# Attention loop of a Perceiver-style block: VectorE forms the low half of the softmax weights in every slot, GpSimd keeps the division and the copies of queries

## The reference, cut to what matters

```python
kv_rope = kv_c * cos + rotate_half(kv_c) * sin          # 4096 x 128, shared by all heads
q_r = einsum('bshq,hqr->bhsr', q_big, W_qr)             # 256 x 64 per head
k_r = einsum('bld,hdr->bhlr', kv_rope, W_kr)            # 4096 x 64 per head
scores = einsum('bhsr,bhlr->bhsl', q_r, k_r)
attn = softmax(scores, axis=-1)
ctx_c = einsum('bhsl,bld->bhsd', attn, kv_rope)         # 256 x 128 per head
```

## Time and profile before

| | before |
|---|---|
| median of 3 runs | 714.37 us (714.17 to 716.49) |
| the profiled execution, its own time | 717.11 us |
| its span, first to last instruction | 715.2 us |
| mean granted TensorE clock | 0.967 of 2.4 GHz |
| TensorE busy | 651.5 us (91%) |
| VectorE busy | 392.3 us (55%) |
| ScalarE busy | 365.5 us (51%) |
| GpSimd busy | 192.4 us (27%) |

### The profile page before, as it was taken

One profiled execution on the slowest core, in us unless ns is written; L12 is line 12 of the kernel. 1 busy time (PEld: TensorE's weight loads), 2 busy tenths in 40 slices (PEclk: granted clock), 3 DMA queues, 4 the chain that ended last, 5 costly groups with the idle time before them and its releaser, 6 DMA issues.

```text
span 715.2 us, 14853 instructions
## 1 busy us (share of the span) xinstructions
PE 651.5 (91%) x5860; PEld 457.7 (64%) x5860; DVE 392.3 (55%) x541; ACT 365.5 (51%) x540; POOL 192.4 (27%) x154
## 2 busy tenths in 40 slices
PE   5899899999999999999999999989978988898457
PEld 4776576777777777777777777985556856632111
DVE  1977677767767767767777675341137836100001
ACT  2453476677666676667577666861217842110000
POOL 2430134343443434344334334440002210000000
PEclk9999999999999999999999999999999989999768
DMA  8914691423324224224306215009970051399990
GB/s 362 418 51 95 144 335 41 108 45 70 77 49 88 49 49 88 53 46 99 76 12 132 51 32 113 2 10 416 417 288 1 0 207 60 136 397 419 416 391 34
DMA packets 25112, 105.13 MB, mean 147 GB/s; under 512 B 3697, under 2 KB 6897, under 8 KB 19185
## 3 DMA queue, kind: packets, MB, share of 16 engines
q1 hardware_dynamic: 25072, 104.57, 44.7%
HBM read 77.29 MB, written 0.52 MB: 109 GB/s over the span
## 4 chain that ended last, share of the span: by engine, by line
PE 61%; DVE 17%; issue 9%; DMA 6%; ACT 4%; SPq 3%; POOL 1%; DVEq 0%; ACTq 0%
DVE arena L748 8%; PE psO L1040 6%; PE psM L989 6%; DMA arena<-w_exp 6%; PE psO L1031 5%; PE psO L1032 5%; PE psS L1018 5%; PE psS L1019 5%; PE psO L1111 4%; DVE arena L711 3%; SPq L374 3%; PE psO L944 3%; PE psO L976 2%; PE psS L1253 2%; PE psO L978 2%
## 5 line engine op out<-in xcount | busy, mean ns | idle before, releaser
L711 DVE TENSOR_REDUCE arena<-psM 128x2 f32<-128x1024 f32 x128 | 156.7, 1224 | 79.4 <-PE psM L989 79.2
L440 POOL TENSOR_TENSOR arena<-arena 128x1024 bf16<-128x1024 f32 x64 | 138.4, 2163 | 144.7 <-ACT arena L539 140.6
L538 ACT ACTIVATE arena<-psS 128x1024 bf16<-128x1024 f32 x128 | 132.2, 1032 | 26.0 <-PE psS L1019 13.8
L1031 PE MATMUL psO<-arena 128*128 128x129 bf16 x1024 | 132.8, 220 | 1.5 <-ACT arena L538 1.2
L539 ACT ACTIVATE arena<-psS 128x1024 f32<-128x1024 f32 x128 | 132.5, 1035 | 0.0
L1032 PE MATMUL psO<-arena 128*128 128x128 bf16 x1024 | 132.3, 220 | 0.0
L1018 PE MATMUL psS<-arena 128*128 128x256 bf16 x512 | 120.5, 273 | 1.4 <-DVE arena L722 1.4
L1019 PE MATMUL psS<-arena 65*128 65x256 bf16 x512 | 120.8, 273 | 0.0
L1031 PEld LDWEIGHTS psO<-arena 128*128 128x128 bf16 x1024 | 99.1, 98 | 20.9 <-issue 12.7
L1032 PEld LDWEIGHTS psO<-arena 128*128 128x128 bf16 x1024 | 99.3, 97 | 6.7
L748 DVE TENSOR_TENSOR arena<-arena 128x1024 bf16<-128x1024 f32 x64 | 82.2, 1285 | 20.7 <-ACT arena L539 20.7
(11 more groups left out here) (192 smaller groups left out, 766.8 us busy)
## 6 DMA issues: line engine op xcount, KB each, us to landing
arena<-w_exp SPq DMA_DIRECT2D x32, 1024.0 KB, 17.3
arena<-arena SPq DMA_DIRECT2D x96, 256.0 KB, 3.8
arena<-w_exp SPq DMA_DIRECT2D x32, 512.0 KB, 17.9
arena<-w_pair SPq DMA_DIRECT2D x8, 1088.0 KB, 16.6
arena<-w_o SPq DMA_DIRECT2D x1, 4096.0 KB, 21.1
arena<-ctx SPq DMA_DIRECT2D x4, 512.0 KB, 13.4
arena<-rope SPq DMA_DIRECT2D x4, 512.0 KB, 14.1
arena<-w_shared_in SPq DMA_DIRECT2D x1, 2048.0 KB, 8.7
```

The lines of the kernel that those rows point to most:

```text
L440: nc.gpsimd.tensor_tensor(p_lo[:, s % 2, :], p_f[:, s % 2, :], p_hi[:, s % 2, :], ALU.subtract).then_inc(s_plo[0], 1)
L538: nc.scalar.activation(p_hi[:, s % 2, :], psS[s % 2][:, :], ACT.Exp).then_inc(s_phi, 1)
L711: nc.vector.reduce_max(maxes[:, :, st, c], psM[:, :].rearrange("p (j n) -> p j n", j=2), AX.X).then_inc(s_mfree, 1)
L1031: mm(psC[:, st, :], ph, vx[:, GROUP * g + i, 0:CW], start=g == 0 and i == 0 and st == 0, stop=False, skip_group_check=True)
```

## The change

GpSimd no longer forms p_lo; VectorE forms it in even slots as well, at the place in its slot where it did so in odd ones, and each parity's semaphore is incremented from there. GpSimd keeps normalise, bring_next and bring, which now follow each other with no p_lo between them. TensorE gets one more wait in slot 0 of a pair: the maximum of keys piece 1 waits for bring's copies by name (it used to be sure of them through the p_lo of slot 14).

```diff
-            def low_part(p, s):
-
-                wait_apart(pool, s_pf, p * SLOTS + s + 1, pool_passed)
-                wait_apart(pool, s_pv, p * SLOTS + s - 1, pool_passed)
-                nc.gpsimd.tensor_tensor(p_lo[:, s % 2, :], p_f[:, s % 2, :], p_hi[:, s % 2, :], ALU.subtract).then_inc(s_plo[0], 1)
...
                     if s == HALF:
                         normalise(p * 2)
-                    low_part(p, s)
                     if after and s == 4:
                         bring_next(p + 2)
...
                     for d, m in maxima[0:1]:
                         maximum(p + d, m)
-                    if s % 2:
-                        dve.wait_ge(s_pf, t + 1)
-                        wait(dve, s_pv, t - 1)
-                        nc.vector.tensor_tensor(p_lo[:, s % 2, :], p_f[:, s % 2, :], p_hi[:, s % 2, :], ALU.subtract).then_inc(s_plo[1], 1)
+                    dve.wait_ge(s_pf, t + 1)
+                    wait(dve, s_pv, t - 1)
+                    nc.vector.tensor_tensor(p_lo[:, s % 2, :], p_f[:, s % 2, :], p_hi[:, s % 2, :], ALU.subtract).then_inc(s_plo[s % 2], 1)
                     for d, c in keys:
                         keys_low(p + d, c)
...
                 if st == 0:
                     pe.wait_ge(s_khi, q * CHUNKS + c + 1)
+                if m == TT and not (isinstance(q, int) and q < 2):
+                    pe.wait_ge(qmax_copied, q * 3 + 3)
```

## The result

The changed kernel takes 725.09 us (median; 723.45 to 727.45), the kernel before 714.27 us beside it: 1.0153 times, 95% interval 1.0111 to 1.0194. That is 10.8 us slower, where 13.8 were forecast; 728.2 us was the forecast time, and 725.1 lies in the range of 720 to 736. One execution of the kernel before (1045.85 us) and one of e3 (1250.09 us) were slow ones and stand in no comparison.

A forecast was written before the change was run, and what follows sets the result against it. A ring of waits between VectorE and TensorE was taken to bound the kernel. ENTRY 4.4, pairs 1 to 5 6.2, pair 6 0.7 and copies 2.5 sum to 13.8 us over the 714.4 median: 728.2 us, range 720 to 736.

The forecast's parts named there:

- the ring: Loop's double slots: VectorE and TensorE wait on each other in 6.31 us; work between even and odd reductions free to 2.89.
- case A: The prediction's own case: VectorE becomes the bound in the late reductions, 11 to 18 us more; chance 0.70.
- Plain double slots: Slots 2, 4, 6 and 10 of a pair: even to odd reduction becomes 2.93 for 2.89 us, taken as +0.03.
- Slots 0 and 8: Slots where a finished head is copied out first: odd reduction at 2.93 for 2.66 us, +0.26, twice per pair.
- Slots 12 to 15: Late slots of a pair: from p_lo of slot 13 to that of slot 15, 6.62 for 6.02 us, +0.6.
- The copies' meeting: Slot 0: GpSimd's bring_next copies delay VectorE's subtraction 0.5 us on five pairs, 2.5 us, from 0 to 3.6.
- ENTRY: First stretch: slots 4 and 6 +0.91 each, 8 and 10 +0.59 each, 0 +0.6, 3 +0.2, 12 to 15 +0.6; 4.4 us.
- Pairs 6 and 7: Last pairs: pair 6, two head slots' terms, four plain ones, no tail, 0.7 us; pair 7, no reductions, 0.
- rival D: Faster: GpSimd is slower, so moving gives back ScalarE's waits and pair 7's two meetings, to 706.6 us; chance 0.06.
- Dispatch: Loop's double slots, pairs 1 to 5: register waits might add 0 to 0.1 us each, up to 4 us; taken 0.
- rival B: VectorE bounds every slot and costs more, with dispatch and all copies going first: 733 to 736 us; chance 0.15.
- Rival C: Loop's double slots absorb the subtraction and the tail; only ENTRY's single psM shows, 3 to 5 us; chance 0.06.

The follow-up runs named there:

- e3: Changed kernel with GpSimd's copies of bring_next after the division of slot 8 rather than in front of it; 725.26 us beside 714.61, ratio 1.0161.
- e1: Kernel before, with VectorE taking the even subtraction only in plain slots 2, 4, 6, 10 of pairs 1 to 6; 714.55 us beside 714.61, ratio 0.9998.
- e2: Changed kernel, but GpSimd keeps the even subtraction in slots 2, 4, 6, 10 of pairs 1 to 6; 725.86 us beside 714.61, ratio 1.0151.
- e5: Changed kernel with VectorE's subtraction ahead of the reduction in odd slots only; 714.39 us beside 713.92, ratio 1.0009.
- e8: e5 plus ScalarE making the high keys of even slots 0 to 10 behind the next slot's exponentials, outside ENTRY; 711.41 us beside 714.41, ratio 0.9965.
- e7: Kernel before, odd subtraction ahead of its reduction, ScalarE's high keys of even slots 0 to 10 behind next slot's exponentials outside ENTRY; 706.26 us beside 714.41, ratio 0.9879.

## Why the prediction was right, and where its terms were off

The mechanism is the one forecast: a subtraction is free where VectorE idled in the ring, and costs in the head slots, the late slots and ENTRY. The cost came out at 10.83 us for 13.8, just under the 11 to 18 that case A named. Of the 3.0 us that are missing the copies are 1.4, the slots of the loop 1.3 and pair 7 0.3.

**Plain double slots, +0.03.** Measured 0.00: the ring stayed at 6.31 us, and e1 confirms it with 24 subtractions at no cost.

**Slots 0 and 8, +0.26 each.** Slot 8 cost 0.21 (272.85 to 279.36 is 6.51 us, before 6.30). Slot 0 cost 0.46, of which 0.22 is the meeting with the copies and 0.24 this term; e2, without the meeting, has 6.52 us there, 0.22 over before.

**Slots 12 to 15, +0.6.** Measured 0.55: p_lo of slot 13 to p_lo of slot 15 is 6.57 us (292.47 to 299.04) for 6.02. The bank for the keys of slot 13, by my own rows, was to be 0.18 us late (284.04 less 283.86) and not 0.23; of the 0.1 that I let TensorE lose by it 0.07 shows, the reduction of slot 14 coming 2.02 us behind the keys for 1.95. These are the changed kernel's rows:

```profile
292.47 1.22 DVE L741 TENSOR_TENSOR arena<-arena 128x1024 bf16<-128x1024 f32 x1
293.62 0.68 DVE L699 TENSOR_TENSOR arena<-psO,arena 128x512 bf16<-128x512 f32 x1
...
295.64 1.23 DVE L705 TENSOR_REDUCE arena<-psM 128x2 f32<-128x1024 f32 x1
296.78 1.22 DVE L741 TENSOR_TENSOR arena<-arena 128x1024 bf16<-128x1024 f32 x1
297.91 1.22 DVE L705 TENSOR_REDUCE arena<-psM 128x2 f32<-128x1024 f32 x1
```

**The copies' meeting, 2.5 us.** This is the term that was mis-sized most, and the largest single part of the miss. The mechanism was there in each of the five pairs, at the forecast place, but it cost 0.22 us each, 1.1 us in all, the lower of the two lengths that the prediction worked out (0.25 behind the first copy alone, 0.72 behind all three). I took the middle, where the rows allowed only one or the other. The Trainium skill's rule ("SBUF — State Buffer", Who interferes with whom) says that whichever of VectorE and GpSimd issues first has the ports that they share for the whole instruction, and the other blocks. The trace agrees: the subtraction, issued during the first copy, took 1.44 us, and the second copy, next behind the subtraction, 1.29 us.

**The loop in sum.** 0.46 + 0.21 + 0.55 is 1.22 us, and a pair grew by 1.20 to 1.21 (50.65 to 51.86), where 1.24 + 0.5 was forecast. In five pairs that is 6.04 us for 8.7. The low end of the range, 720, lies 3.5 us under the 723.5 that its own sum of 9.1 gives; the measured 725.1 is above both.

**ENTRY, 4.4 us.** Measured 4.37, and not by luck: the reduction of slot 2 came 0.77 us later for the 0.6 of slot 0's keys, slot 3 added 0.24 for 0.2, slots 4 and 6 0.86 each for 0.91, slots 8 and 10 some 0.55 each for 0.59, and slots 12 to 15 0.55 for 0.6. In slot 4 the second reduction comes 2.87 us after the first (before 2.01), and slot 5's 0.49 behind its end, as forecast:

```profile
100.61 1.23 DVE L705 TENSOR_REDUCE arena<-psM 128x2 f32<-128x1024 f32 x1 [1.08 <-PE psM L984]
101.75 1.22 DVE L741 TENSOR_TENSOR arena<-arena 128x1024 bf16<-128x1024 f32 x1
102.88 0.68 DVE L699 TENSOR_TENSOR arena<-psO,arena 128x512 bf16<-128x512 f32 x1
103.48 1.22 DVE L705 TENSOR_REDUCE arena<-psM 128x2 f32<-128x1024 f32 x1
105.19 1.23 DVE L705 TENSOR_REDUCE arena<-psM 128x2 f32<-128x1024 f32 x1 [0.49 <-PE psM L984]
```

**Pairs 6 and 7.** 0.72 for 0.7 in pair 6 is luck in good part. Its two head slots cost 0.17 us each for 0.26, its plain slots nothing for 0.12, and 0.37 us came between the p_lo of slot 13 and the bias row of slot 14 (2.70 us for 2.33), where I had put nothing. e2 does not have them (2.34), and no run shows why. Pair 7 got 0.30 us shorter, which I had counted as nothing. It takes 37.17 or 37.18 us in the four kernels in which GpSimd subtracts there, and 36.87 to 36.89 in all others. So the two meetings of the earlier trace rows, at which rival D put 1.8 us each if they were on the path, seem to have cost some 0.3 us together.

**Dispatch, 0 to 0.1 us per double slot.** It is 0, as taken: in the loop the reduction starts 0.61 us after the keys (258.49 to 259.10), with waits on registers. That rules out most of rival B.

**The clock and the new wait.** The clock stayed at 1.00 through the loop, and TensorE's waits show nothing on the copies. e1 and e5 have the same new wait, and the time of the kernel before.

**Rival C** (3 to 5 us) fell: the idle time was real and took in the subtractions of the plain slots in full, but it was not where the head slots and the late slots need it. **Rival D** (faster) fell, too. GpSimd's subtraction is slower, 2.13 us to 1.22, and "GPSIMD Engine Reference", 4.1 Engine selection, of the Trainium skill would have it on VectorE. Here nobody on the ring waited for it. But e8 shows that a kernel with all the subtractions on VectorE can be faster than the one before, once the order is mended, though e7, with GpSimd's help, stays ahead.

Four marks that I named were off. The subtraction in slot 0 took 1.44 us, not 1.5 to 2.0. The head slots took 6.51 and, with the meeting, 6.76 us, not 6.6. VectorE is busy 456 us, not near 470. In pairs 1 to 5 the 40 new subtractions are 48.8 us of work and added 41.2 us of busy time, since back-to-back instructions overlap by 0.06 to 0.09 us and busy time counts that once. In pair 7, where VectorE's subtractions no longer meet GpSimd's (2.98 us for 1.22), the eight new ones added 6.0 us for 9.8. GpSimd is busy 61 us, not 56: five copies took 1.29 us for 0.29.

## What to carry to other kernels

Before giving an engine more work, find the ring of waits that sets the pace, and add up what the engine does between its two meetings with the other engine. A free share of 29% said nothing here; 2.89 us between two reductions, against 2.93 of work by the sum (2.90 as it came out), said it to a few hundredths. If such a ring holds, look first at the order within it: turning two instructions round and moving a third gave 8 us, while moving the subtractions alone cost 11 us and, in the mended order, cost 5 us (e8 less e7).

## What I had not expected

- A row of instructions on one engine can be broken into. GpSimd issued three copies back to back, and VectorE's waiting subtraction got in after the first; the second, a 0.29 us copy, then took 1.29 us.
- The same code behind the loop took from 230.5 to 236.5 us in different executions. One cause shows in the windows. The clock granted just after the loop was 0.83 before the change (first row) and 1.00 after it (second row), so that TensorE had part of the first stretch at the lower of its two levels. It is not the change that does this. From the last head copy to VectorE's fifth copy out of psM behind it, seven of the eleven profiles took 10.90 or 10.91 us, with a clock of 1.00 over the first 12.4 us. The other four took 12.14 to 12.46 us with 0.86, and one of these is the second profile of the changed kernel itself (12.14). The kernel before took 12.38, which is 1.47 of the 1.54 us by which its rest is longer. The DMA share of the stretch is alike in all of them (0.91 to 0.93).

```profile
480.00:490.00 10.00, 8.03 (x30) 4.96 (x31) 2.13 (x6) 1.39 (x4) 0.61 (x1) 0.83 0.81 310
```
```profile
490.00:500.00 10.00, 7.83 (x37) 4.65 (x37) 2.61 (x7) 1.76 (x5) 0.61 (x1) 1.00 0.78 305
```
